# Two AdaLN-like layers, their first three tiles in another order: W0 and x loaded first, the second layer's operands split before the first mixing, late mix blocks copied by ScalarE, no products of ones

## The chip, the cores and the metric

The kernel runs on one core of a Trainium2 chip. The metric is the time on the device of one execution, in microseconds (us). TensorE (PE) multiplies, VectorE (DVE), ScalarE (ACT) and GpSimd (POOL) do the rest, SyncE (SP) issues nearly all DMAs. Every engine works its own list of instructions in order; what they wait for on each other are semaphores written out by hand. All numbers are fp32; where a product needs fp32 accuracy, each operand is split into a high and a low part (type fp32r), and a product is made as hi*hi + hi*lo + lo*hi.

## The reference

Two layers, each adds to x [128, 32, 512] what a feed-forward part makes of a conditioned x:

```
x = x + ffn0(cond0(x))
x = x + ffn1(cond1(x))
cond0: att = softmax(MLP(cond_128));  agg_w[b] = sum_k att[b,k] weight[k]  (32x32 per batch row)
       out[b] = agg_w[b] @ x[b] + (att @ bias_k)[b]
ffn0:  x @ W_base.T + b_base + rank-8 terms of 4 active experts, weighted by a softmax of router logits
cond1: grouped convolution over the 512 positions (9 taps, 4 groups) + (cond_128 @ c_weight.T) + bias
ffn1:  x @ base_W.T + rank-8 terms of the best 2 of 28 experts, weighted by a softmax
```

## The kernel before

**Tiles.** 128 batch rows x 32 channels are 32 tiles of 128 rows (4 batch rows each) and 512 columns. Because `cond0` mixes only within a batch row, the kernel multiplies first and mixes later: `u = x @ [A0 | W0]` per tile (`u_half`, line 1018; half "a" has 292 columns: 36 of the router and rank-8 weights `a0` and 256 of W0, half "b" the other 256), then `mixing` (line 1096) multiplies u by `mix`, a 128x128 block-diagonal matrix of the four `agg_w`. A half of u is 12 products: 8 with x's high part (lines 996, 997) and 4 with its low part (line 1002).

**Steps.** `steps` runs a function `step(s)` on each engine for s = 0 to 33. Step s holds the mixing of tile s, u of a tile further on, the convolution of tile s-1 (`conv`), and layer 2 of tile s-2 (`lows_1`, `base_1`) and s-3 (`low_rank_1`). Steps 0, 1 and 2 are written out apart, step 3 and later are one form. In front of step 0 stands a prologue on every engine:

- SP (lines 361 to 394) loads in this order: `pack` (cond_128, the MLP's weights), `active`, `kw`, x of tile 0, the four chunks of W0, `rows_a`, x of tiles 1 and 2, then four register loads each followed by a DMA of B0's rows, `b_base`, and, when W0 is split (`w0_lo_done`), W1 into the same buffer `w_sb`, `a1`, and so on.
- PE (lines 1028 to 1092): 5 products of ones, the MLP of `cond_128` (`u1_mm`, `u2_mm`, `am_mm`) with `keep_busy` between, which is products of ones again, 18 in all; half b of u of tile 0 chunk by chunk (`first_chunk`) as W0's chunks come; attention, `beta0`; the 8 products `p_mix` that make all `agg_w` (line 1077; 16 passes, since fp32 takes two); column sums of W0 (lines 1008, 1009), half a, more sums, half b of tile 1. Half a of tile 1 stands in step 0, behind the first mixing.
- DVE and ACT share the splits: ACT makes the high part (a cast), DVE the low part (a subtraction). Both copy the blocks of `p_mix` into `mix` for tiles 0 to 3 (`mix_copies`, lines 546 and 739).
- The other 28 tiles' blocks: ACT copies `p_mix` whole to `mix_raw` (`raw_copied`, step 0), POOL copies 16 blocks from there (line 496, steps 1 and 2). POOL also makes the constant rows of the second window buffer (line 463), `z_add` of the 28 tiles (lines 474, 478) and the low part of `b1` (line 513).
- The second layer's operands are split late: `a1` and the first half of W1 in step 1, `b1` and the second half of W1's low part in step 2.

**What links a tile to the next layer.** `residual` (line 827, DVE) makes x1 of a tile; SP stores it (line 417), then loads three shifted windows of it into `win` (line 403); `conv` waits for these.

## Time and profile before

| | us |
|---|---|
| median of 3 runs (390.02 to 390.41) | 390.1 |
| the profiled execution | 389.76 |
| its span, first to last instruction | 388.0 |
| PE busy in it | 376.9 (97%) |
| DVE, ACT, POOL busy | 276.4, 121.1, 41.7 |

The profile is of one execution. Each row of the timeline is an instruction, or several alike one behind the other, with its start, its duration, the operation and what it writes and reads; behind it in brackets the idle time in front of it and what ended that. A product's duration includes the time to run through the array, so products overlap: their pitch is read from start to start. Times at POOL are rough. The span leaves out 1.76 us around the program.

### The profile page before, as it was taken

Reading aid. Unit: us, or ns where it says so; the run is one execution under the profiler, and the core shown is the slowest. Engines: PE = TensorE matmul, PEld = TensorE weight load, DVE = VectorE, ACT = ScalarE, POOL = GpSimd, SP = SyncE. Lnnn points to the kernel's source line nnn. Section 1 sums busy time; section 2 is a strip of 40 time slices with the busy share of each in tenths; the row PEclk is TensorE's granted clock in tenths of the full one; section 3 lists DMA queues with packets and bytes.
Section 4 is the critical chain, followed back from the end, with each engine's and each line's share of the span. In section 5 each row is a group of like instructions: output and inputs, shape, how many; then the busy total and the mean of one; then the engine's idle time right before and its main releaser. Section 6 shows DMA issues by size and latency. Waiting matters only on the chain.

```text
span 388.0 us, 9591 instructions
## 1 busy us (share of the span) xinstructions
PE 376.9 (97%) x3183; PEld 331.3 (85%) x3183; DVE 276.4 (71%) x937; ACT 121.1 (31%) x379; POOL 41.7 (11%) x114
## 2 busy tenths in 40 slices
PE   8999899999999999999999999999999999998986
PEld 7999778888898888888988888889888888887674
DVE  6678997666776676667767767677677666776754
ACT  5266432322333223223332232233322322222211
POOL 2636720000000000000000000000000000000000
PEclk9999999999999999999999999999999999999999
DMA  6765647667777656677776656767766566676631
GB/s 216 256 182 122 161 134 194 175 154 183 162 190 182 141 149 168 153 182 162 190 179 139 157 160 155 187 162 190 180 136 160 160 159 155 139 175 156 164 80 54
DMA packets 71018, 63.05 MB, mean 163 GB/s; under 512 B 4030, under 2 KB 53502, under 8 KB 70872
## 3 DMA queue, kind: packets, MB, share of 16 engines
q1 hardware_dynamic: 70998, 62.82, 64.7%
q8 instruction: 10, 0.16, 0.2%
q14 instruction: 8, 0.07, 0.1%
q10 hardware_dynamic: 2, 0.00, 0.0%
HBM read 45.75 MB, written 16.91 MB: 162 GB/s over the span
## 4 chain that ended last, share of the span: by engine, by line
PE 89%; DVE 5%; DMA 3%; issue 1%; ACT 1%; SPq 1%; DVEq 0%; ACTq 0%
PE p_chy L996 14%; PE p_chy L1002 14%; PE p_chy L997 14%; PE p_u L996 9%; PE p_u L997 8%; PE p_u L1002 8%; PE p_chy L1141 8%; PE p_t L1153 3%; PE p_y L996 2%; PE p_y L1002 2%; PE p_y L997 2%; DMA win<-x_scratch 1%; DMA w_sb<-in_w 1%; PE p_y L1125 1%; PE p_chy L1077 1%
## 5 line engine op out<-in xcount | busy, mean ns | idle before, releaser
L996 PE MATMUL p_u<-w_hi,xt_hi 128*128 128x256 f32 (+1 forms) x256 | 70.5, 302 | 0.8 <-DVE w_lo L729 0.5
L997 PE MATMUL p_u<-w_lo,xt_hi 128*128 128x256 f32 (+1 forms) x256 | 68.1, 292 | 0.0
L835 DVE STREAM_TRANSPOSE c<-p_chy 128x512 f32<-128x512 f32 x32 | 22.9, 716 | 54.2 <-PE p_chy L1141 54.2
L544 ACT CAST u_hi<-p_u 128x256 fp32r<-128x256 f32 x64 | 24.9, 389 | 106.0 <-PE p_u L1002 106.0
L996 PEld LDWEIGHTS p_u<-w_hi,xt_hi 128*128 128x128 f32 x256 | 49.3, 192 | 1.5 <-issue 1.5
L593 ACT CAST g1t_hi<-p_t 112x256 fp32r<-112x256 f32 x32 | 11.9, 373 | 120.7 <-PE p_t L1153 120.7
L997 PEld LDWEIGHTS p_u<-w_lo,xt_hi 128*128 128x128 f32 x256 | 49.4, 193 | 0.0
L996 PE MATMUL p_chy<-w_hi,c_hi 128*128 128x512 f32 x124 | 49.3, 397 | 0.0
L997 PE MATMUL p_chy<-w_lo,c_hi 128*128 128x512 f32 x124 | 48.8, 394 | 0.0
L1002 PE MATMUL p_u<-w_hi,xt_lo 128*128 128x256 f32 (+1 forms) x256 | 43.0, 290 | 0.0
L1002 PEld LDWEIGHTS p_u<-w_hi,xt_lo 128*128 128x128 f32 x256 | 36.6, 190 | 0.0
L1141 PEld LDWEIGHTS p_chy<-win,wc_sb 100*32 100x32 f32 x1024 | 26.0, 109 | 12.3 <-issue 10.6
L1141 PE MATMUL p_chy<-win,wc_sb 100*32 100x128 f32 x1024 | 34.6, 276 | 1.2 <-DMA win<-x_scratch 1.1
L1002 PE MATMUL p_chy<-w_hi,c_lo 128*128 128x512 f32 x124 | 34.0, 396 | 0.0
L996 PE MATMUL p_chy<-a_hi,c_hi 128*128 128x252 f32 x128 | 31.4, 279 | 0.0
L997 PE MATMUL p_chy<-a_lo,c_hi 128*128 128x252 f32 x128 | 31.3, 279 | 0.0
L736 DVE TENSOR_TENSOR u_lo<-p_u,u_hi 128x256 fp32r<-128x256 f32 x64 | 25.6, 434 | 4.4 <-ACT u_hi L544 4.4
L1002 PEld LDWEIGHTS p_chy<-w_hi,c_lo 128*128 128x128 f32 x124 | 23.1, 188 | 5.3
L996 PEld LDWEIGHTS p_chy<-w_hi,c_hi 128*128 128x128 f32 x124 | 23.3, 188 | 4.5 <-issue 0.2
L997 PEld LDWEIGHTS p_chy<-w_lo,c_hi 128*128 128x128 f32 x124 | 23.3, 188 | 4.0
L507 POOL COPY wc_sb<-beta_rows 4x128 f32 (+1 forms) x32 | 9.8, 307 | 154.8 <-PE p_chy L1141 154.5
L996 PE MATMUL p_chy<-b_hi,g1t_hi 112*128 112x512 f32 x62 | 24.9, 402 | 1.4 <-ACT g1t_hi L593 1.4
(166 smaller groups left out, 761.9 us busy)
## 6 DMA issues: line engine op xcount, KB each, us to landing
win<-x_scratch SPq DMA_DIRECT2D x96, 256.0 KB, 4.4
x_scratch<-x SPq DMA_DIRECT2D x32, 260.0 KB, 2.1
xt_sb<-in_xt SPq DMA_DIRECT2D x32, 256.0 KB, 5.1
x_sb<-in_x SPq DMA_DIRECT2D x32, 256.0 KB, 5.1
out<-y_sb SPq DMA_DIRECT2D x32, 256.0 KB, 4.3
w_sb<-in_w SPq DMA_DIRECT2D x4, 256.0 KB, 4.9
w_sb<-in_w SPq DMA_DIRECT2D x1, 1024.0 KB, 5.9
a_sb<-in_a SPq DMA_DIRECT2D x1, 504.0 KB, 7.0
```

The costliest lines, as they stand in the source:

```text
L507: pool.tensor_copy(wc_sb[KIM:KC, s.mod(2)].rearrange("b g (r o) -> b g r o", r=NPH), beta1_rows[KIM:KC, s.n(), :].rearrange("b (g o) -> b ...
L544: nc.scalar.copy(u_hi[:, t.mod(4), cols], p_u[:, banks]).then_inc(u_hi_done[half], 1)
L593: nc.scalar.copy(g1t_hi[:], p_g1t).then_inc(g1t_hi_done, 1)
L736: V.tensor_tensor(u_lo[:, t.mod(4), cols], p_u[:, banks], u_hi[:, t.mod(4), cols].bitcast(f32), ALU.subtract).then_inc(u_lo_done[half], 1)
L835: V.transpose(c1[:], p_cv).then_inc(c1_tr, 1)
L996: mm(psum, lhs_hi, rhs_hi, start=start and n == 0, stop=False)
L997: mm(psum, lhs_hi, rhs_lo, start=False, stop=False)
L1002: last = mm(psum, lhs_lo, rhs_hi, start=False, stop=stop and n == len(operands) - 1)
L1077: last = mm(p_mix[:, m * BATCH:(m + 1) * BATCH], kw_sb[:, m * BT * CH:(m + 1) * BT * CH], att_t[:], start=True, stop=True)
L1125: mm(p_y0[:, ZA + Z0N:ZB], g0t[:], b0_stack[:, 0:NY], start=False, stop=True, skip_group_check=True)
L1141: last = mm(p_cv[rows, :].rearrange("p (b g m) -> p b g m", b=BT, g=GROUPS)[:, :, g], wc_sb[:, v.mod(2), g, :], win[:, v.mod(2)].rearrange ...
L1153: last = nc.tensor.transpose(p_g1t[:, a, :], g1[:, a, :], ident[:])
```

## The change

It moves work in the prologue and in steps 0 to 2; the form of step 3 and later stays.

- Loads: x of tile 0 and W0 first on SP's queue, `pack` on ACT's queue ahead of the router's load; `a1` and `b1` early, W1 as soon as W0 is split; B0's rows, x of tile 0 and `beta1_rows` behind it.
- PE: no products of ones; the MLP's products between W0's chunks; half a of tile 0 ahead of the attention; column sums and `p_mix` behind it; both halves of tile 1 ahead of step 0.
- ACT: splits of `a1`, `b1` and half of W1 in the prologue, copies of the 28 tiles' blocks straight from `p_mix` (`mix_late`, 16 copies of 32 x 224 in steps 0, 1 and 2).
- DVE: low parts of `a1` and `b1` in the prologue, both halves of W1's in step 1, the second window buffer's constant rows in step 2, `z_add` of the 28 tiles at the end of step 2.
- POOL: keeps clearing `mix` (now in one go behind `a0` and `vact`), and two small copies per step.
- `lows_1` of tile 0, which overwrites `p_mix`, waits for the late copies; the convolution of tile 1 and not of tile 0 waits for the constant rows.

The diff, cut (8 columns of indentation taken off):

```diff
 
-    sp.dma_start(pack_sb[:], pack).then_inc(ld_pack, 16)
-    sp.dma_start(act_sb[:], active).then_inc(ld_act, 16)
-    sp.dma_start(kw_sb[:], kw).then_inc(ld_kw, 16)
     load_xt(0)
     for c in W0_ORDER:
         load_w0(c)
+    sp.dma_start(act_sb[:], active).then_inc(ld_act, 16)
     sp.dma_start(rows_sb[:], rows_a.rearrange("p (c e n) -> p c e n", c=HC, e=E0)).then_inc(ld_rows_a, 16)
     load_xt(1)
+    sp.dma_start(kw_sb[:], kw).then_inc(ld_kw, 16)
+    sp.dma_start(a1_sb[:], a1.rearrange("p (c n) -> p c n", c=HC)).then_inc(ld_a1, 16)
     load_xt(2)
+    sp.dma_start(b1_sb[:], b1.rearrange("p (a d) -> p a d", a=2)).then_inc(ld_b1, 16)
+    sp.wait_ge(w0_lo_done, HC)
+    sp.dma_start(w_sb[:], w1.rearrange("p (c d) -> p c d", c=HC)).then_inc(ld_w1, 16)
     sp.wait_ge(ld_act, 16)
...
     sp.dma_start(x_sb[:, 0, :], x_v[0]).then_inc(x_loaded[0], 16)
-    sp.wait_ge(w0_lo_done, HC)
-    sp.dma_start(w_sb[:], w1.rearrange("p (c d) -> p c d", c=HC)).then_inc(ld_w1, 16)
-    sp.dma_start(a1_sb[:], a1.rearrange("p (c n) -> p c n", c=HC)).then_inc(ld_a1, 16)
     load_xt(3)
     sp.wait_ge(ld_rows_b, 16 * ACT0)
     for n in range(1, 3):
         sp.dma_start(b0_raw[n * L0N:(n + 1) * L0N], b0_raw[0:L0N]).then_inc(copied_b, 16)
+    sp.dma_start(x_sb[:, 1, :], x_v[1]).then_inc(x_loaded[1], 16)
+    sp.wait_ge(xt_lo_done, 1)
+    load_xt(4)
     sp.wait_ge(beta1_done, 1)
     for b in range(BT):
         sp.dma_start(beta1_rows[KIM + b:KIM + b + 1], beta1[b:BATCH:BT, :]).then_inc(beta1_moved, 16)
-    sp.dma_start(x_sb[:, 1, :], x_v[1]).then_inc(x_loaded[1], 16)
-    sp.wait_ge(xt_lo_done, 1)
-    load_xt(4)
     for n in range(2):
         sp.dma_start(wc_sb[0:KIM, n], wc.rearrange("k (g n) -> k g n", g=GROUPS)).then_inc(ld_wc, 16)
-    b1_v = b1.rearrange("p (a d) -> p a d", a=2)
-    sp.dma_start(b1_sb[:], b1_v).then_inc(ld_b1, 16)
...
-    zero_mix(range(0, 3))
...
-    pool.wait_ge(ident_done, 1)
-    pool.tensor_copy(win[KIM:KC, 1].rearrange("k (b g) q -> k b (g q)", g=GROUPS),
-                     ident[KIM:KC, KIM:KC].unsqueeze(2).to_broadcast([BT, BT, GROUPS * NQ])).then_inc(batch_rows_done, 1)
-    pool.wait_ge(batch_rows_done, 1)
-    zero_mix(range(3, NT // UNROLL))
-
...
+    zero_mix(range(NT // UNROLL))
...
-            if at(s, 1):
-                pool.wait_ge(raw_act_done, 2)
-                pool.wait_ge(mix_zeroed, NT // UNROLL)
-            if at(s, 1) or at(s, 2):
-                pool.wait_ge(g0_beta_done, s.c + 1)
-                for n in range(2 * s.c - 2, 2 * s.c):
-                    for b in range(BT):
-                        pool.tensor_copy(*raw_blocks(n, b)).then_inc(mix_rest_done, 1)
-                        pool.wait_ge(mix_rest_done, n * BT + b + 1)
-        if at(s, 0):
-            z_rows_rest()
...
-        if at(s, 1):
-            pool.wait_ge(b1_hi_done, 1)
-            pool.wait_ge(wc_beta_done, 2)
-            pool.tensor_tensor(b1_lo[:], b1_sb[:], b1_hi[:].bitcast(f32), ALU.subtract).then_inc(b1_lo_done, 1)
...
+    act.dma_start(pack_sb[:], pack).then_inc(ld_pack, 16)
     act.dma_start(rt_sb[:], router.rearrange("p (a e) -> p a e", a=2)).then_inc(ld_rt, 16)
...
+    def mix_late(n):
+
+        for b in range(BT):
+            nc.scalar.copy(*mix_blocks(REST, n, b)).then_inc(mix_rest_done, 1)
...
     nc.scalar.activation(m1[:], p_mlp, ACT.Gelu, bias=pack_sb[:, C_B0:C_B0 + 1]).then_inc(m1_done, 1)
+    first, second, third = (Tile(None, t) for t in range(3))
+    w0_high(1)
     act.wait_ge(u2_mm, 1)
     nc.scalar.activation(m2[:], p_mlp, ACT.Gelu, bias=pack_sb[:, C_B1:C_B1 + 1]).then_inc(m2_done, 1)
-    act.wait_ge(am_max_done, 1)
-    nc.scalar.activation(am_exp[:], am[:], ACT.Exp, bias=am_max[:], accum_out=am_sum[:]).then_inc(am_exp_done, 1)
-    w0_high(1)
     w0_high(3)
-    first, second, third = (Tile(None, t) for t in range(3))
     xt_high(second)
     act.wait_ge(a0_done, ACT0)
     nc.scalar.copy(w0_hi[:, :, 0:Z0N], a0[:]).then_inc(a0_hi_done, 1)
+    act.wait_ge(am_max_done, 1)
+    nc.scalar.activation(am_exp[:], am[:], ACT.Exp, bias=am_max[:], accum_out=am_sum[:]).then_inc(am_exp_done, 1)
     u_high(first, "b")
-    act.wait_ge(mix_zeroed, 1)
+    act.wait_ge(ld_a1, 16)
+    nc.scalar.copy(a1_hi[:], a1_sb[:]).then_inc(a1_hi_done, 1)
+    act.wait_ge(ld_b1, 16)
+    nc.scalar.copy(b1_hi[:], b1_sb[:]).then_inc(b1_hi_done, 1)
+    u_high(first, "a")
+    xt_high(third)
+    w1_high(0)
+    act.wait_ge(mix_zeroed, NT // UNROLL)
     act.wait_ge(mix_mm, 1)
     mix_copies(FIRST, range(BT // 2))
-    u_high(first, "a")
     mix_high(first)
-    act.wait_ge(rsw0_mm, 1)
-    nc.scalar.copy(b0_raw[3 * L0N:3 * L0N + 3, NY:D], p_rsw0["b"][3 * L0N:3 * L0N + 3]).then_inc(rsw0b_done, 1)
-    xt_high(third)
     u_high(second, "b")
     act.wait_ge(rs0_done, 1)
     nc.scalar.copy(b0_raw[3 * L0N:3 * L0N + 3, 0:NY], p_rsw0["a"][3 * L0N:3 * L0N + 3]).then_inc(rsw0_done, 1)
+    act.wait_ge(rsw0_mm, 1)
+    nc.scalar.copy(b0_raw[3 * L0N:3 * L0N + 3, NY:D], p_rsw0["b"][3 * L0N:3 * L0N + 3]).then_inc(rsw0b_done, 1)
     act.wait_ge(rsw0_done, 1)
     act.wait_ge(rsw0b_done, 1)
     act.wait_ge(ld_rows_b, 16 * ACT0)
     act.wait_ge(copied_b, 16 * 4)
     nc.scalar.copy(b0_round[:], b0_raw[:]).then_inc(b0_round_done, 1)
+    u_high(second, "a")
...
         if at(s, 0):
             z0_exponent(s)
-            raw_copied(0)
-            u_high(s + 1, "a")
+            mix_late(0)
+            u_high(s + 2, "b")
             xt_high(s + 3)
-            u_high(s + 2, "b")
             g0t_copied(s)
-            raw_copied(1)
             u_high(s + 2, "a")
+            mix_late(1)
             xt_high(s + 4)
             mix_high(s + 2)
         elif at(s, 1):
             u_high(s + 2, "b")
             z0_exponent(s)
             u_high(s + 2, "a")
-            act.wait_ge(ld_a1, 16)
-            nc.scalar.copy(a1_hi[:], a1_sb[:]).then_inc(a1_hi_done, 1)
+            w1_high(1)
             xt_high(s + 4)
             u_high(s + 3, "b")
-            w1_high(0)
+            mix_late(2)
             u_high(s + 3, "a")
             g0t_copied(s)
             mix_high(s + 2)
-            w1_high(1)
         elif at(s, 2):
             u_high(s + 3, "b")
-            act.wait_ge(ld_b1, 16)
-            nc.scalar.copy(b1_hi[:], b1_sb[:]).then_inc(b1_hi_done, 1)
+            mix_late(3)
             c1_high(s + -LAG)
             u_high(s + 3, "a")
             z0_exponent(s)
             xt_high(s + 4)
+            mix_high(s + 2)
             t_exponent(s + -LAG)
             g0t_copied(s)
-            act.wait_ge(mix_zeroed, NT // UNROLL)
-            mix_high(s + 2)
...
-    dve.wait_ge(ld_pack, 16)
     w0_high(0, 1)
     w0_low(0)
+    w0_high(2, 2)
+    w0_low(2)
+    xt_low(first)
+    dve.wait_ge(w0_hi_act, 1)
+    w0_low(1)
+    dve.wait_ge(w0_hi_act, 2)
+    w0_low(3)
+    dve.wait_ge(ld_pack, 16)
+    dve.wait_ge(beta1_mm, 1)
+    V.tensor_tensor(beta1[:], p_beta1, pack_sb[:, C_FS:C_FS + CH], ALU.add).then_inc(beta1_done, 1)
     dve.wait_ge(am_mm, 1)
     V.tensor_tensor(am[:], p_am, pack_sb[:, C_B2:C_B2 + MK], ALU.add).then_inc(am_done, 1)
     dve.wait_ge(am_done, 1)
     V.tensor_reduce(am_max[:], am[:], X, ALU.max, negate=True).then_inc(am_max_done, 1)
-    w0_high(2, 2)
-    w0_low(2)
-    xt_low(first)
-    dve.wait_ge(beta1_mm, 1)
-    V.tensor_tensor(beta1[:], p_beta1, pack_sb[:, C_FS:C_FS + CH], ALU.add).then_inc(beta1_done, 1)
+    xt_low(second)
+    dve.wait_ge(a0_hi_done, 1)
+    V.tensor_tensor(w0_lo[:, :, 0:Z0N], a0[:], w0_hi[:, :, 0:Z0N].bitcast(f32), ALU.subtract).then_inc(a0_lo_done, 1)
     dve.wait_ge(am_exp_done, 1)
     V.reciprocal(am_rec[:], am_sum[:]).then_inc(am_rec_done, 1)
     dve.wait_ge(am_rec_done, 1)
     V.tensor_scalar(att[:], am_exp[:], am_rec[:], None, ALU.mult).then_inc(att_done, 1)
-    dve.wait_ge(w0_hi_act, 1)
-    w0_low(1)
+    u_low(first, "b")
     dve.wait_ge(att_t_mm, 1)
     V.tensor_copy(att_t[:], p_att).then_inc(att_t_done, 1)
-    dve.wait_ge(w0_hi_act, 2)
-    w0_low(3)
+    dve.wait_ge(a1_hi_done, 1)
+    V.tensor_tensor(a1_lo[:], a1_sb[:], a1_hi[:].bitcast(f32), ALU.subtract).then_inc(a1_lo_done, 1)
     dve.wait_ge(beta0_mm, 1)
     V.tensor_copy(beta0[:], p_beta0).then_inc(beta0_done, 1)
+    dve.wait_ge(b1_hi_done, 1)
+    V.tensor_tensor(b1_lo[:], b1_sb[:], b1_hi[:].bitcast(f32), ALU.subtract).then_inc(b1_lo_done, 1)
+    u_low(first, "a")
     dve.wait_ge(beta0_done, 1)
...
-    xt_low(second)
-    dve.wait_ge(a0_hi_done, 1)
-    V.tensor_tensor(w0_lo[:, :, 0:Z0N], a0[:], w0_hi[:, :, 0:Z0N].bitcast(f32), ALU.subtract).then_inc(a0_lo_done, 1)
-    u_low(first, "b")
-    dve.wait_ge(mix_zeroed, 1)
-    dve.wait_ge(mix_mm, 1)
-    mix_copies(FIRST, range(BT // 2, BT))
-    u_low(first, "a")
-    mix_low(first)
     dve.wait_ge(vrow_mm, 1)
     V.tensor_copy(vrow[:], p_vrow).then_inc(vrow_done, 1)
     dve.wait_ge(zrow_mm, 1)
     V.tensor_copy(rs0[:], p_rs0).then_inc(rs0_done, 1)
+    dve.wait_ge(mix_zeroed, NT // UNROLL)
+    dve.wait_ge(mix_mm, 1)
+    mix_copies(FIRST, range(BT // 2, BT))
+    mix_low(first)
+    u_low(second, "b")
     dve.wait_ge(rs0_done, 1)
     dve.wait_ge(vrow_done, 1)
     z_rows(FIRST, 1)
-    u_low(second, "b")
...
-            dve.wait_ge(a1_hi_done, 1)
-            V.tensor_tensor(a1_lo[:], a1_sb[:], a1_hi[:].bitcast(f32), ALU.subtract).then_inc(a1_lo_done, 1)
+            w1_low(0)
             u_low(s + 3, "a")
-            w1_low(0)
+            w1_low(1)
         elif at(s, 2):
             u_low(s + 3, "b")
             residual(s + -1)
             c1_transposed(s + -LAG)
-            w1_low(1)
+            V.tensor_copy(win[KIM:KC, 1].rearrange("k (b g) q -> k b (g q)", g=GROUPS),
+                          ident[KIM:KC, KIM:KC].unsqueeze(2).to_broadcast([BT, BT, GROUPS * NQ])).then_inc(batch_rows_done, 1)
             c1_low(s + -LAG)
             z0_logits(s)
             u_low(s + 3, "a")
...
+            z_rows(REST, 2)
+            dve.wait_ge(z_add_done, 2)
...
     pe.wait_ge(ones_done, 1)
-    for _ in range(5):
-        mm(p_u[:, 0:P], ones[:], ones[:], start=True, stop=True)
-
-    pe.wait_ge(ones_r_done, 1)
-
-    def keep_busy(n):
-
-        for _ in range(n):
-            mm(p_u[:, 0:P], ones_r[:], ones_r[:], start=True, stop=True)
-
-    pe.wait_ge(ld_pack, 16)
...
     after(pe, xt_hi_done, first)
     first_chunk(0)
-    keep_busy(6)
+    pe.wait_ge(ld_pack, 16)
+    mm(p_mlp, pack_sb[:, C_W0:C_W0 + P], cond, start=True, stop=True).then_inc(u1_mm, 1)
+    mm(p_beta1, cond, pack_sb[:, C_CW:C_CW + CH], start=True, stop=True).then_inc(beta1_mm, 1)
     first_chunk(1)
-    keep_busy(4)
+    pe.wait_ge(m1_done, 1)
+    mm(p_mlp, pack_sb[:, C_W1:C_W1 + P], m1[:], start=True, stop=True).then_inc(u2_mm, 1)
+    first_chunk(2)
+    first_chunk(3)
+    pe.wait_ge(m2_done, 1)
+    mm(p_am, m2[:], pack_sb[:, C_W2:C_W2 + MK], start=True, stop=True).then_inc(am_mm, 1)
+    after(pe, xt_lo_done, first)
+    lo_passes(p_u[:, banks], u_operands(first, cols), True).then_inc(u_mm["b"], 1)
+    pe.wait_ge(a0_lo_done, 1)
+    u_half(first, "a")
     pe.wait_ge(ident_done, 1)
     pe.wait_ge(att_done, 1)
     nc.tensor.transpose(p_att, att[:], ident[:]).then_inc(att_t_mm, 1)
-    first_chunk(2)
+    pe.wait_ge(vact_done, ACT0)
+    mm(p_vrow, ones[0:1, :], vact[:], start=True, stop=True).then_inc(vrow_mm, 1)
     pe.wait_ge(ld_kw, 16)
     pe.wait_ge(att_t_done, 1)
     for b in range(BT):
         last = mm(p_beta0[by_batch[b]], kw_sb[:, CH * CH:CH * CH + CH],
                   att_t[:].rearrange("k (t b) -> k b t", b=BT)[:, b, :], start=True, stop=True)
     last.then_inc(beta0_mm, 1)
+    pe.wait_ge(ones_r_done, 1)
+    pe.wait_ge(beta1_done, 1)
+    _, cols = HALVES["a"]
+    column_sums(p_cv[:, 0:Z0N + NY], P, w0_hi[:, :, cols], w0_lo[:, :, cols]).then_inc(zrow_mm, 1)
     for m in range(CH // BT):
         last = mm(p_mix[:, m * BATCH:(m + 1) * BATCH], kw_sb[:, m * BT * CH:(m + 1) * BT * CH], att_t[:],
                   start=True, stop=True)
     last.then_inc(mix_mm, 1)
-    first_chunk(3)
-    after(pe, xt_lo_done, first)
-    lo_passes(p_u[:, banks], u_operands(first, cols), True).then_inc(u_mm["b"], 1)
+    u_half(Tile(None, 1), "b")
     pe.wait_ge(beta0_done, 1)
+    _, cols = HALVES["b"]
     column_sums(p_rsw0["b"], P, w0_hi[:, :, cols], w0_lo[:, :, cols]).then_inc(rsw0_mm, 1)
-    pe.wait_ge(a0_lo_done, 1)
-    u_half(first, "a")
-    pe.wait_ge(vact_done, ACT0)
-    mm(p_vrow, ones[0:1, :], vact[:], start=True, stop=True).then_inc(vrow_mm, 1)
-    pe.wait_ge(beta1_done, 1)
-    _, cols = HALVES["a"]
-    column_sums(p_cv[:, 0:Z0N + NY], P, w0_hi[:, :, cols], w0_lo[:, :, cols]).then_inc(zrow_mm, 1)
-    u_half(Tile(None, 1), "b")
+    u_half(Tile(None, 1), "a")
...
-                pe.wait_ge(batch_rows_done, 1)
                 pe.wait_ge(batch_rows_0, 1)
                 pe.wait_ge(rsw0_done, 1)
+            if at(v, 1):
+                pe.wait_ge(batch_rows_done, 1)
...
-                pe.wait_ge(raw_act_done, 2)
+                pe.wait_ge(mix_rest_done, MIX_REST)
...
             mixing(s)
-            u_half(s + 1, "a")
             u_half(s + 2, "b")
```

## Rows read from the trace of the kernel before

**Rows 1.** The page, part 1: busy time, share of the span and instructions of each engine.
```profile
PE 376.9 (97%) x3183; PEld 331.3 (85%) x3183; DVE 276.4 (71%) x937; ACT 121.1 (31%) x379; POOL 41.7 (11%) x114
```

**Rows 2.** Stretches: bounds, length; busy (instructions) of PE, PEld, DVE, ACT, POOL; clock; DMA.
```profile
24.60:52.00 27.40, 25.25 (x227) 22.59 (x226) 25.43 (x61) 15.04 (x39) 17.84 (x26) 1.00 0.53 130
52.00:340.00 288.00, 287.91 (x2512) 254.72 (x2516) 204.84 (x730) 86.00 (x285) 12.23 (x51) 1.00 0.67 165
```

**Rows 3.** Timeline of PE, 24 to 53 us: start, duration, line, names, shapes, count.
```profile
24.67 0.30 PE L996 MATMUL p_y<-u_hi,mix_hi 128*128 128x292 f32 x1
...
25.43 0.30 PE L996 MATMUL p_u<-w_hi,xt_hi 128*128 128x292 f32 x1
...
39.81 1.08 PE L1141 MATMUL p_chy<-win,wc_sb 100*32 100x128 f32 x32
...
52.09 0.40 PE L996 MATMUL p_y<-u_hi,mix_hi 128*128 128x292 f32 x1 [0.16 <-DVE x L827]
```

**Rows 4.** Timeline of PE, 0 to 24.6 us.
```profile
1.07 2.50 PE L1030 MATMUL p_u<-ones 128*128 128x128 f32 x10 [1.07 <-DVE ones L692]
...
12.44 3.78 PE L1077 MATMUL p_chy<-att_t,kw_sb 8*128 8x128 f32 x16
...
16.74 1.05 PE L1002 MATMUL p_u<-w_hi,xt_lo 128*128 128x256 f32 x4
17.59 0.41 PE L1008 MATMUL p_t<-w_hi,ones_r 128*128 128x256 f32 x1
...
19.30 0.45 PE L996 MATMUL p_u<-w_hi,xt_hi 128*128 128x292 f32 x1
...
21.00 0.30 PE L997 MATMUL p_u<-w_lo,xt_hi 128*128 128x292 f32 x1
...
24.20 0.64 PE L1002 MATMUL p_u<-w_hi,xt_lo 128*128 128x256 f32 x4
```

**Rows 5.** Timeline of DVE, 3 to 21 us.
```profile
3.89 1.22 DVE L702 COPY win<-ident 4x2048 f32<-4x2048 f32 x1
...
6.98 0.43 DVE L724 CAST w_hi<-w_sb 128x512 fp32r<-128x512 f32 x1 [1.30 <-DMA w_sb<-in_w]
7.44 0.69 DVE L729 TENSOR_TENSOR w_lo<-w_sb,w_hi 128x512 fp32r<-128x512 f32 x1
...
18.69 1.95 DVE L743 COPY mix<-p_chy 32x32 f32<-32x32 f32 x8
```

**Rows 6.** Timeline of ACT, 18 to 20 us.
```profile
18.10 1.82 ACT L550 COPY mix<-p_chy 32x32 f32<-32x32 f32 x8
```

**Rows 7.** Timeline of DVE, 39 to 45 us.
```profile
39.04 1.22 DVE L749 TENSOR_TENSOR w_lo<-w_sb,w_hi 128x1024 fp32r<-128x1024 f32 x1
...
40.51 0.68 DVE L827 TENSOR_TENSOR x<-p_y,x_sb 128x512 f32<-128x512 f32 x1
...
41.74 2.75 DVE L749 TENSOR_TENSOR w_lo<-w_sb,w_hi 128x1024 fp32r<-128x1024 f32 x1
```

**Rows 8.** Waits, 0 to 60 us: engine, line, releaser; total us, times, longest.
```profile
PE p_chy L1002 <- DVE c_lo L840: 0.8, 1, 0.8
...
PE p_t L1153 <- DVE g L965: 0.5, 1, 0.5
...
PE p_t L1118 <- DVE g0s L871: 0.4, 1, 0.4
...
PEld p_chy L1141 <- DMA win<-x_scratch: 0.3, 1, 0.3
```

**Rows 9.** Timeline of POOL, 29 to 44 us.
```profile
29.75 5.79 POOL L496 COPY mix<-mix_raw 32x224 f32<-32x224 f32 x8 [0.45 <-ACT mix_raw L626]
...
41.00 2.40 POOL L513 TENSOR_TENSOR b_lo<-b_sb,b_hi 112x1024 fp32r<-112x1024 f32 x1 [5.05 <-ACT b_hi L655]
```

**Rows 10.** Timeline of SP, 6 to 32 us: DMA issues and register loads.
```profile
6.86 4.26 SPq L373 DMA_DIRECT2D b_raw<-in_rows_b  x4
...
31.37 0.35 SPq L417 DMA_DIRECT2D x_scratch<-x  x1
```

48 lines of the change are left out of this document (6 added, 42 removed).

## The prediction

> **What bounds the kernel now.** I read the page first, then the stretches, then the products in order of time up to 60 us, then DVE, ACT, POOL and the DMA queue over the same time. The page says that PE is busy 97% of the span [rows 1]. The stretches say where the other 3% are: from 52 to 340 us PE works 287.91 of 288.00 us, between 24.6 and 52 us only 25.25 of 27.40 [rows 2]. The diff leaves the loop's steps 3 and later untouched, and they are a line of products with nothing between them. So the change is worth what it does to one number, the moment at which the mixing of tile 3 starts: 52.09 us [rows 3]. A microsecond gained there is a microsecond gained at the end.
>
> Up to that moment there are two stretches. I call T0 the start of the mixing of tile 0 (24.67 us), and the way from T0 to the mixing of tile 3 the climb: 52.09 - 24.67 = 27.42 us [rows 3].
>
> In the stretch up to T0, PE looks busy, but at which speed? The products tell it. Four of 256 columns start at 16.74 us and the next product at 17.59, so the pitch is 0.85/4 = 0.213 us: 256 columns at 1.2 GHz. Four at 24.20 us are followed at 24.67 [rows 3], 0.118 us each: the 2.4 GHz level. The step lies at 21.00 us, where one of 292 columns takes 0.30 us and not 0.45 [rows 4]. Before it, PE had run products of 256 and 292 columns one behind the other since the mixing passes' end at 12.44 + 3.78 = 16.2 us; these are 16 passes with only 8 rows, and before them it ran mainly products of ones, the first at 1.07 us [rows 4].
>
> **Part 1: the products of ones go.** They lie in time in which PE would wait for W0, and 15 us of them brought no higher clock before 16 us [rows 4]. I take 0 for them. The Trainium skill (TensorE: Matmul & The Clock Gate, Part 1) holds that the array starts throttled and that activity releases it, which speaks against taking them out; the rows disagree, since activity of this kind released nothing. By the page the higher level would come later without them, as in the first of the rivals below.
>
> **Part 2: W0 and x first.** DVE waited until 6.98 us for the first chunk of W0, and its split ended at 7.44 + 0.69 = 8.13 us [rows 5]. Ahead of that chunk stood pack, kw and x, by their shapes in the code 233 + 33 + 256 KB; now x and, on ACT's queue, pack, 256 + 233 KB: nearly the same bytes, so I take 0.1 us. The Trainium skill (DMA: Bandwidth & Descriptors, Issuing engines are not separate DMA queues) says that queues of several engines share the same DMA engines, so that a second queue saves issue time alone; by it this edit gains nothing by the queue. The router's load now stands behind pack on ACT's queue, and DVE waits for it first, with the copy into win (1.22 us, [rows 5]) and the split of x behind; up to 1.3 us of that is covered by the wait that DVE has there today [rows 5]. The chunks 1 and 3 are split by ACT behind the two Gelu steps, whose products now follow the first chunks; with two products and two splits for each I work out the last split at 11.9 us.
>
> **Part 3: the order of PE up to T0.** The first half of u (12 products) starts now at 19.30 us [rows 4]. In front of it stood the 16 mixing passes, 3.78 us, and 8 column sums of 0.213, 1.70 us; both move behind it, so it starts at about 14.1 (19.30 - 5.48 = 13.8, and 0.3 for the attention's steps on DVE, which now stand ahead of the split of a0 that this half waits for). From there PE does, in order, each at the lower or the higher level: the half, 12 products of 292 columns, 2.92 us; attention to beta0, small transposes and copies, some 0.95; 8 column sums, 1.95 or 1.07; mixing passes, 3.78 or about 1.9 (half, an estimate); the next tile's half b, 12 x 0.213 = 2.56 or 1.43; column sums, 1.70 or 0.96; its half a, which before stood behind T0 at 25.43 [rows 3], 2.92 or 12 x 0.134 = 1.60. All low this is 16.8 us, all high behind the first half 10.8.
>
> Everything hangs on when the clock steps up, and the trace of before can't show it. Bounds: if the dense stretch from about 12.8 to 17.1 us is enough, T0 = 14.1 + 10.8 = 24.9; if it comes during the column sums, at 20, they are 0.9 dearer: 25.8. If the step comes as long behind the last mixing pass as in before, 16.2 to 21.0, 4.8 us, the passes end at 14.1 + 2.92 + 0.95 + 1.95 + 3.78 = 23.7 and it comes at 28.5: half b and the sums run low (until 27.95), half a begins low, T0 = 29.8. I take 25.4, the middle of the first two: what PE did before the step of before, products of full width one behind the other, it does here from about 12.8 us on, with breaks of 0.5 and 1 us.
>
> What must be hidden for that: the mix copies that T0 needs (8 on ACT in 1.82 us, 8 on DVE in 1.95, [rows 5, 6]) follow the mixing passes, that end near 21.5; with mix_high and mix_low T0 could be 24.0, so PE has 1 us or more to give. Queued in front of those copies are, on ACT, the splits of a1, b1 and half of w1. The half of w1 waits for 1 MB that is issued once the last split of W0 is done; if it lands later than 20 us, the copies and T0 move with it. A third wait is new in its place: SP's four register loads with their DMAs (4.26 us, [rows 10]), the rows of B0, their copies, x of tile 0 and 1 and beta1 now stand behind w1, and ACT's b0_round waits for the copies with half a of tile 1 queued behind it. From w1's issue at 12 us that is 16.6 for the last load, and by two landings of some 3 us, 23 for the copies; ACT comes there near 25. On DVE stand a1_lo and b1_lo, 1.2 us each by the like split of W1 [rows 7], while PE does its column sums.
>
> **Part 4: the climb.** Removed: half a of tile 1, 1.60 us. Removed with POOL's work: PE waited 0.8 us for c_lo, 0.5 for g and 0.4 for g0s [rows 8]. Why: a split of 1024 columns on DVE takes 1.22 us, but 2.75 when POOL's b_lo (2.40 us from 41.00) runs beside it [rows 7, 9]. It ends 1.09 us after POOL's: it waited. The Trainium skill (SBUF - State Buffer, two separate sides) calls the pair of ports an exclusive lock between the two; the rows agree. In its place between transpose and c_lo comes the copy into win, 1.22 us as in [rows 5]. At the end of step 2, z_rows for 28 tiles comes to DVE, about 1.4 us by [rows 7]; PE covers it as long as it is itself late for the reason that follows.
>
> Added: a new wait. Convolution 0 starts when win has landed: the residual's store is issued at 31.37 and the convolution came at 39.81 after a wait of 0.3 [rows 3, 8, 10], so 8.4 us from store to products. Without half a PE comes 1.6 us earlier, win does not. The residual of tile 0 is done near T0 + 5.65 (its store is now issued at T0 + 6.7; PE's 1.6 us less, but DVE's chain to g0s is 0.5 us longer than what PE does meanwhile) and convolution 0 starts at T0 + 14.1. The residual of tile 1, now started at 40.51 = T0 + 15.84 [rows 7], ended at T0 + 16.5; DVE's work up to it stays (the second split of W1 comes in place of a1's), less 1 us of waits on POOL, so it ends near T0 + 15.5. By the same 8.4 us convolution 1 starts at T0 + 24.0 though PE is ready at T0 + 22.1; then transposes, and the mixing of tile 3 at T0 + 25.4. So the climb shrinks by 2.0 us, not by the 3.3 that the removed work and waits add up to. Bounds: 1.6 (only half a goes) to 3.3 (win lands in time).
>
> The 16 late copies on ACT (32 x 224): no row shows one. Lower bound 0.23 us, from 1.82/8 at 32 columns [rows 6]; upper 0.72, POOL's 5.79/8 for the same blocks [rows 9]. I take 0.35, nearer to ACT's own row. That is 5.6 us on an engine busy 15.04 of 27.40 us there [rows 2], which at the same time gives up the splits of a1, b1 and half of W1. At 0.72 the copy of g0t in step 0 would come some 0.5 us late.
>
> **Sum.** Mixing of tile 3 at 25.4 + 25.4 = 50.8, against 52.09: 1.3 us. The profiled execution took 389.76 us (span 388.0), so 388.5; the median of the runs, 390.1, is 0.34 above it, so 388.8.
>
> **The rivals.**
> - *The clock stays low through the mixing passes (slower).* T0 = 29.8, and with the same climb of 25.4 the mixing of tile 3 starts at 55.2, 3.1 us later: 393.2. For it: in before the clock was low from the first pass to the last and 4.8 us on [rows 4], and now fewer full products stand ahead of the passes than then stood behind them. Against: then the passes came first, and no row shows what a run of full products does before them. It decides from the point at which the clock is still low when the mixing passes begin and stays so to their end.
> - *The step comes at about 21 us, as now (same).* 5 of the 16 passes low, T0 = 26.4, mixing of tile 3 at 51.8, 0.3 us earlier: 389.8. For it: the gains of order are then eaten by slower products.
> - *The climb has no new wait.* T0 = 24.9, climb 24.1, mixing of tile 3 at 49.0: 387.0. For it: win's landing varies; against: the wait of 0.3 us in [rows 8] shows that there is no slack.
>
> **How the numbers follow.** Forecast 0.42, slower rival 0.36, same 0.14, large gain 0.08. This kernel's runs tell about 0.2% (0.8 us) from no change. The forecast's own range is 387.8 to 389.7 (T0 24.9 to 25.8, climb 24.9 to 25.9), of which 0.36 lies beyond 0.2% and 0.06 within; the same-rival gives 0.10 within and 0.02 to each side; the slow rival 0.35 slower and 0.01 within. Faster 0.36 + 0.08 + 0.02 = 0.46, same 0.17, slower 0.37. The range must reach to the slow rival: 387.2 to 393.4.
>
> **What would show it.** Right: first half of u near 14 us; pitch 0.12 us in the column sums or the mixing passes; T0 near 25; c_lo and g0s no longer named as what PE waits for; win named in front of the convolution of tile 1. Wrong: a pitch of 0.213 us still at 24 us; T0 bounded by mix copies or by the load of w1; DVE's first work held up by the router's load behind pack.

## The result: 1.6% slower, and where it went

The changed kernel takes 395.97 us (median of runs from 394.06 to 398.77) where the kernel before, run beside it, takes 390.2: a ratio of 1.016, with an interval from 1.0129 to 1.0191. The forecast was 388.8 us and the range ended at 393.4, so the prediction is wrong in its sign and in its range. The profiled execution took 395.63 us. Its three moments, from [rows 3] and the rows below:

| us | before | after | forecast |
|---|---|---|---|
| T0, mixing of tile 0 | 24.67 | 30.47 | 25.4 |
| mixing of tile 3 (the climb) | 52.09 (27.42) | 56.97 (26.50) | 50.8 (25.4) |
| from there to the last instruction | 335.91 | 336.83 | 335.91 |

Ratios leave out the runs in the chip's slower state (three of e4's ten and two of e7's), while medians and ranges hold all runs.

The page of after, part 1, against [rows 1]: PE works less, POOL much less, and the span is 5.8 us longer.

```profile
span 393.8 us, 9526 instructions
## 1 busy us (share of the span) xinstructions
PE 374.6 (95%) x3155; PEld 328.4 (83%) x3155; DVE 271.5 (69%) x941; ACT 128.7 (33%) x393; POOL 24.3 (6%) x94
```

The timeline of PE in after (start, duration, line, what is written and read, count, in brackets the wait and what ended it), to be read beside [rows 3, 4]: line 1029 is the mixing passes, 952 and 953 the products of u and the mixing.

```profile
14.06 0.61 PE L952 MATMUL p_u<-w_hi,xt_hi 128*128 128x292 f32 x1 [0.22 <-DVE w_lo L733]
...
20.54 3.78 PE L1029 MATMUL p_chy<-att_t,kw_sb 8*128 8x128 f32 x16
...
28.46 0.41 PE L965 MATMUL p_t<-w_lo,ones_r 128*128 128x256 f32 x1
28.68 0.45 PE L952 MATMUL p_u<-w_hi,xt_hi 128*128 128x292 f32 x1
28.92 0.38 PE L953 MATMUL p_u<-w_lo,xt_hi 128*128 128x292 f32 x1
29.13 0.30 PE L952 MATMUL p_u<-w_hi,xt_hi 128*128 128x292 f32 x1
...
30.47 0.30 PE L952 MATMUL p_y<-u_hi,mix_hi 128*128 128x292 f32 x1
...
40.41 0.35 PE L952 MATMUL p_u<-w_hi,xt_hi 128*128 128x256 f32 x1 [0.89 <-DVE u_lo L687]
...
55.77 1.08 PE L1086 MATMUL p_chy<-win,wc_sb 100*32 100x128 f32 x32 [1.45 <-DMA win<-x_scratch]
...
56.97 0.38 PE L952 MATMUL p_y<-u_hi,mix_hi 128*128 128x292 f32 x1
...
59.53 0.73 PE L958 MATMUL p_chy<-b_hi,g1t_lo 112*128 112x512 f32 x2 [0.63 <-DVE g1t_lo L801]
```

The first half of u starts at 14.06 us, as forecast. Then the passes take 3.78 us, the price of before, and the step from 0.45 to 0.30 us, from 1.2 to 2.4 GHz, comes at 29.0 us, 4.7 us behind their end: in before it was 4.8. From 14.06 us to T0 PE waits for no operand, and up to 29.0 it runs at half its clock. The profile's granted clock reads 1.00 over this stretch in both kernels, though the pitch is that of 1.2 GHz; so a level ahead of the first step is read from the pitch, and the granted clock tells later falls. In the climb PE waits for u_lo (0.89 us) and win (1.45), and just behind it for g1t_lo (0.63), where it waited for c_lo, g and g0s [rows 8].

### The profile page after: what moved, and what is told of

Its sections match the earlier page's. It is cut to its first block, busy times and chain, and to the rows that moved or that the text cites. A ratio compares the mean times of both kernels' runs of the same rounds, so it can differ in the third digit from the quotient of the medians.

```text
span 393.8 us, 9526 instructions
## 1 busy us (share of the span) xinstructions
PE 374.6 (95%) x3155; PEld 328.4 (83%) x3155; DVE 271.5 (69%) x941; ACT 128.7 (33%) x393; POOL 24.3 (6%) x94
## 4 chain that ended last, share of the span: by engine, by line
PE 86%; DVE 6%; DMA 3%; ACT 3%; issue 2%; SPq 0%; ACTq 0%; DVEq 0%
PE p_chy L952 14%; PE p_chy L958 14%; PE p_chy L953 14%; PE p_u L952 9%; PE p_u L953 8%; PE p_u L958 8%; PE p_chy L1086 7%; PE p_t L1098 3%; PE p_y L952 2%; PE p_y L958 2%; PE p_y L953 2%; DMA win<-x_scratch 1%; ACT mix L516 1%; PE p_chy L1029 1%; PE p_y L1069 1%
## 5 line engine op out<-in xcount | busy, mean ns | idle before, releaser
L952 PE MATMUL p_u<-w_hi,xt_hi 128*128 128x256 f32 (+1 forms) x256 | 71.9, 307 | 9.8 <-DVE w_lo L680 8.5
L953 PE MATMUL p_u<-w_lo,xt_hi 128*128 128x256 f32 (+1 forms) x256 | 69.0, 295 | 0.0
L952 PEld LDWEIGHTS p_u<-w_hi,xt_hi 128*128 128x128 f32 x256 | 49.9, 195 | 11.5 <-issue 9.4
L494 ACT CAST u_hi<-p_u 128x256 fp32r<-128x256 f32 x64 | 24.9, 388 | 96.5 <-PE p_u L958 96.4
L560 ACT CAST g1t_hi<-p_t 112x256 fp32r<-112x256 f32 x32 | 11.9, 373 | 122.9 <-PE p_t L1098 122.9
L958 PE MATMUL p_u<-w_hi,xt_lo 128*128 128x256 f32 (+1 forms) x256 | 44.2, 296 | 0.0
L958 PEld LDWEIGHTS p_u<-w_hi,xt_lo 128*128 128x128 f32 x256 | 37.5, 195 | 0.0
L952 PE MATMUL p_chy<-b_hi,g1t_hi 112*128 112x512 f32 x62 | 24.9, 402 | 1.4 <-ACT g1t_hi L560 1.4
L953 PEld LDWEIGHTS p_chy<-a_lo,c_hi 128*128 128x128 f32 x128 | 24.2, 189 | 1.3
```

Source lines behind the costliest of these rows:

```text
L494: nc.scalar.copy(u_hi[:, t.mod(4), cols], p_u[:, banks]).then_inc(u_hi_done[half], 1)
L560: nc.scalar.copy(g1t_hi[:], p_g1t).then_inc(g1t_hi_done, 1)
L952: mm(psum, lhs_hi, rhs_hi, start=start and n == 0, stop=False)
L953: mm(psum, lhs_hi, rhs_lo, start=False, stop=False)
L958: last = mm(psum, lhs_lo, rhs_hi, start=False, stop=stop and n == len(operands) - 1)
```

## The experiments

Each was timed beside the kernel before; a time is the median, then the range, then the ratio to before with its interval. A run's own T0 and climb are those of its profile, which is one execution. The diffs are cut, with `...` where lines are left out.

**Products of ones, as they were.** e1 puts them back into after, e2 takes them out of before.

```diff
+            keep_busy(8)
             cond = pack_sb[:, C_COND:C_COND + BATCH]
...
             first_chunk(0)
+            keep_busy(6)
...
             first_chunk(1)
+            keep_busy(4)
```

> The changed kernel with the 5 + 18 products of ones put back (13 ahead of W0's first chunk, 6 behind the first chunk, 4 behind the second). Theory P (the place of the mixing passes keeps the clock low: the step comes some 4.8 us behind the last of them): the clock still steps up near 29 us, the time stays near that of the changed kernel, 395 to 397, 15 or so products of ones more in front cost at most 1 us. Theory O (taking out the products of ones keeps the clock low): the step comes before 24 us and the time falls to 392 or below.

e1: 397.15 us (396.39 to 397.93), 1.0178 (1.0138 to 1.0218), the step at 30.7 us, T0 32.38.

```diff
-            keep_busy(6)
             first_chunk(1)
-            keep_busy(4)
```

> The kernel before without any product of ones. Theory P: no change, 389.8 to 390.6, the clock steps up near 21 us as before, because the mixing passes lie where they lay. Theory O: slower by 2 us or more, with the step later than 24 us.

e2: 390.77 us (389.58 to 393.49), 1.0024 (1.0001 to 1.0047), T0 25.28. What follows: these products, of 128 columns, are worth 0.6 us of T0 in before (one profile each), and in after they only delay. That they are gone is not the loss.

**The order of PE.** e3 moves the passes and the attention in after ahead of half a of tile 0, as in before.

```diff
             last.then_inc(beta0_mm, 1)
+            for m in range(CH // BT):
+                last = mm(p_mix[:, m * BATCH:(m + 1) * BATCH], kw_sb[:, m * BT * CH:(m + 1) * BT * CH], att_t[:],
...
+            pe.wait_ge(a0_lo_done, 1)
+            u_half(first, "a")
```

> The changed kernel with the 16 mixing passes moved ahead of half a of tile 0 (and the attention with them), so that behind them products of full width run unbroken. Theory P: passes end near 19 us, the clock steps up near 24, the mixing of tile 0 starts near 28 and not 30.5, so 2 to 3 us less than the changed kernel: 392.5 to 394. Theory O: the step comes no sooner than 28 us, the time stays within 1 us of the changed kernel.

e3: 396.38 us (395.21 to 396.79), 1.0164 (1.0128 to 1.02). The passes start at 16.60, 4 us earlier, the step comes at 23.8, T0 at 28.67. So the step moves with the passes, though not at a fixed distance: 3.4 us behind their end here, 4.7 in after, about 6 in e2. But most of the 1.8 us was lost again in the climb (27.83): PE waited 1.79 us for win ahead of the convolution of tile 1, and its granted clock was 0.50 from 54.6 to 58.0, behind that wait. Five more profiles show the same dip there (e4, e5, e6, e9 and e14, waits of 1.57 to 1.89 us); those of after, e1, e7 and e8 do not, with 1.45, 1.72, 1.80 and 1.30. What decides it stays open.

**The clock raised early.** e4 puts 16 products of ones of 512 columns ahead of the first chunk in after.

```diff
+            for _ in range(16):
+                mm(p_u[:, 0:D], ones_r[:, 0:P], ones_r[:], start=True, stop=True)
             cond = pack_sb[:, C_COND:C_COND + BATCH]
```

> The changed kernel with 16 products of ones of 512 columns each from 1.4 us on, where PE else waits for W0. Theory W (it is the width: products of 128 columns leave PE's array idle while weights load, those of 512 do not): the clock steps up near 6 us, all products up to 30 us run at the higher level, T0 falls from 30.5 to 22 to 25 us: 387 to 391. If the clock falls back in the breaks between 8 and 14 us, T0 stays near 30 and the time within 1 us of the changed kernel. Theory P says as much as the second of these.

e4: 393.85 us (389.08 to 395.96), 1.0047 (1.0006 to 1.0087). In the profiled execution (395.03 us) the level is high from 8 us, falls at 17.6, comes back at 27.8: T0 28.98. Ahead of the fall PE had waited 1.03 us for att, because of a step of DVE (its timeline):

```profile
13.59 2.34 DVE L738 TENSOR_SCALAR att<-am_exp,am_rec 128x8 f32<-128x8 f32 x1
```

Here it ends as POOL's memsets of mix end (12.12 to 15.90 us). In after they run at the same place (12.06 to 15.86) and it takes 0.35 us. e7 therefore adds to e4 that all memsets come before the first rows.

```diff
+            zero_mix(range(NT // UNROLL))
             pool.wait_ge(ld_act, 16)
...
-            zero_mix(range(NT // UNROLL))
```

> After, with 16 products of ones of 512 columns ahead of the first chunk of W0, and all of POOL's memsets of mix moved to the time before the first rows land, so that PE's break of 1.03 us in front of the attention's transpose (DVE's att took 2.34 us beside the memsets) goes. Theory C (T0 is late because PE runs at 1.2 GHz to 29 us, and the high level, once there, stays as long as PE has no break): the products keep a pitch of 0.12 us through the column sums and the mixing passes, T0 comes at about 25 us (30.47 in after), and the time is about 390.5. Rival (the mixing passes with 8 rows themselves bring the low level): pitch 0.21 us behind the passes, T0 28.5 or later, time 394 or more.

e7: 395.35 us (390.56 to 397.65), 1.0101 (1.0065 to 1.0136), T0 28.00. With the memsets done by 6.25 us, att takes 0.23 us. The clock fell once from 11.8 to 18.7, PE waiting for W0's splits ahead of that. Then the rival held: the passes take 2.31 us, mostly at the high level, and the clock falls again, at 22.1.

**The climb.** e5 moves three steps of DVE in after; e6 moves four late copies of ACT behind what PE needs sooner; e8 is e5, e6 and e7 together.

```diff
                     u_low(s + 2, "a")
+                    z_rows(REST, 2)
                     xt_low(s + 4)
...
+                    residual(s)
                     w1_low(1)
...
-                    residual(s + -1)
```

> After, with three DVE steps moved and nothing else: the copy into win ahead of the mix copies, z_rows of the 28 late tiles into step 0 (where DVE waits 2.11 us for ACT), the residual of tile 1 ahead of the second split of W1. Theory W (in the climb new waits took the place of the removed ones): PE's wait for win ahead of the convolution of tile 1 falls from 1.45 us to about 0.4, that for g1t_lo from 0.63 us to 0, and the time falls by 1.4 to 1.8 us, to about 394.4. Rival (the waits only stand where PE would wait for something else anyway): other waits appear in the same place, the time stays within 0.5 us of after.

e5: 394.59 us (392.87 to 396.81), 1.0094 (1.0067 to 1.0121), T0 30.28. The wait for g1t_lo is gone, that for win is 1.72. The store was issued 1.31 us earlier (47.81 in after), and the windows' loads no more than 0.44 (49.89), as the queue of SP shows: the store took longer to land, and so did the windows. The median came out near the 394.4 us that theory W gave, but its mechanism did not: the profile (396.81 us) has a climb of 27.41, with the dip in it, so the number is no evidence for it.

```profile
46.50 0.34 SPq L406 DMA_DIRECT2D x_scratch<-x  x1
49.45 1.39 SPq L392 DMA_DIRECT2D win<-x_scratch  x3
```

```diff
-                    mix_late(1)
                     xt_high(s + 4)
                     mix_high(s + 2)
+                    mix_late(1)
```

> After, with ACT's second set of four late mix copies (2.30 us) moved behind the split of x and mix_high of step 0. If the copies' size on ACT is what PE waits for at 40.41 us (0.89 us for u_lo, DVE behind ACT's split of x), that wait goes, and if nothing later takes it up the time falls by 0.9 us. Rival: the wait for win ahead of the convolution of tile 1 grows from 1.45 us by what is gained, since its chain hangs on DVE's work and not on PE's: time unchanged. I lean to the rival, with 0.3 us gained.

e6: 396.45 us (392.71 to 398.55), 1.017 (1.0124 to 1.0217). The wait for u_lo halves (0.44), one for g0t of 0.26 is new, that for win is 1.78: the rival's case. Its profile shows more than was asked. Up to T0 its instructions are those of after, and yet (PE's timeline; 964 and 965 are the column sums):

```profile
18.17 0.40 PE L964 MATMUL p_chy<-w_hi,ones_r 128*128 128x292 f32 x1
18.41 0.29 PE L965 MATMUL p_chy<-w_lo,ones_r 128*128 128x292 f32 x1
...
19.44 2.05 PE L1029 MATMUL p_chy<-att_t,kw_sb 8*128 8x128 f32 x16
21.42 0.48 PE L952 MATMUL p_u<-w_hi,xt_hi 128*128 128x256 f32 x1
21.70 0.41 PE L953 MATMUL p_u<-w_lo,xt_hi 128*128 128x256 f32 x1
...
24.69 0.41 PE L965 MATMUL p_t<-w_lo,ones_r 128*128 128x256 f32 x1
24.90 0.32 PE L964 MATMUL p_t<-w_hi,ones_r 128*128 128x256 f32 x1
...
27.02 0.30 PE L952 MATMUL p_y<-u_hi,mix_hi 128*128 128x292 f32 x1
```

In this execution the high level came at 18.2 us, as I had forecast, and the passes took 2.05 us and not 3.78. Then the clock fell, at 21.6, and came back at 25.0. The same instructions thus have a T0 of 30.47 or of 27.02, and the times of after spread over 4.7 us. The profiles of e5 and e14, with the same products up to T0, have the late step (28.7 to 28.8 us) as after has. The Trainium skill (TensorE: Matmul & The Clock Gate, What's actually happening) says that the moment of the step varies between runs of one kernel; these two traces agree, but the page gives ±500 ns for it, and here the steps lie 10.8 us apart.

> The three before together. If C and W both hold, T0 is about 25 us, the mixing of tile 3 starts about 24.8 us behind it at 49.8, against 52.09 in before, and the time is about 388. If the high level is lost at the passes (rival of C): about 392.5. If a break of PE ahead of the convolution of tile 1 brings the low level for some 3 us, 1.5 us more than either.

e8: 392.69 us (389.6 to 394.8), 1.0052 (1.0018 to 1.0086). T0 29.01, climb 25.88: the climb gained 0.6 us on after, the clock fell at 21.0, within the passes, all the same.

**The late mix.** e11 makes this part alone, on before; e14 takes it alone out of after.

```diff
-                    raw_copied(0)
+                    mix_late(0)
...
-                                pool.tensor_copy(*raw_blocks(n, b)).then_inc(mix_rest_done, 1)
```

> Before, with the late mix alone changed: ACT copies the 16 blocks straight out of PSUM and POOL copies none (b_lo and z_rows stay with POOL, the prologue stays). The prediction's prices (0.35 us a copy, waits for g and g0s gone): the climb falls from 27.42 us to about 26.5, time 389.3. With 0.57 us a copy as the profile of after shows, ACT's splits of x and u come later and PE waits some 0.9 us for u_lo in step 0 in place of the waits for g and g0s: climb 27.4, time 390.2.

e11: 395.81 us (395.25 to 396.51), 1.014 (1.0123 to 1.0157), both expectations missed by over 5 us. T0 is 24.54, the climb 32.9, with the clock at 0.5 from 51.2 to 54.6. PE's waits in it, 24 to 60 us (engine, line, releaser; total, times, longest):

```profile
PE p_y L979 <- DVE x L810: 1.7, 1, 1.7
PE p_chy L985 <- DVE c_lo L823: 1.6, 1, 1.6
PE p_y L1108 <- ACT g0t L589: 1.5, 1, 1.5
PE p_u L979 <- ACT xt_hi L506: 1.5, 1, 1.5
```

ACT has the copies beside the splits of a1, b1 and W1 here; in after those of a1, b1 and half of W1 stand ahead of T0. e14:

```diff
-                    mix_late(1)
+                    raw_copied(1)
...
+                                pool.tensor_copy(*raw_blocks(n, b)).then_inc(mix_rest_done, 1)
```

> After, with the late mix as in before (ACT copies PSUM to mix_raw in two pieces of 0.6 us, POOL does the 16 blocks); the rest of after stays. If ACT's copies are what kept the climb at 26.5 us, PE's wait of 0.89 us for u_lo in step 0 goes and the climb falls to about 25.6, less what POOL's copies beside DVE's short steps cost (waits of 0.4 to 0.5 us for g0s and g in before). Rival: the chain to win bounds the climb, 26.5 us whoever copies. The time itself follows T0, which in after lies anywhere from 27 to 30.5 us by the clock.

e14: 392.81 us (391.22 to 395.47), 1.0081 (1.0055 to 1.0108). T0 30.29, climb 26.16, the wait for u_lo 0.36, that for win 1.57. So in after the copies on ACT cost the climb some 0.3 us, win takes up the rest. The time fell by more, but T0's scatter lies in it, so what is owed to the copies stays open.

**The passes woven.** e9 is e7 with two full products behind each two passes; e10 does this in before, whose products of ones it also makes 512 wide (and all of type fp32r); e12 has these wide products alone.

```diff
+                for m in range(CH // BT):
+                    last = mm(p_mix[:, m * BATCH:(m + 1) * BATCH], kw_sb[:, m * BT * CH:(m + 1) * BT * CH], att_t[:],
...
+                    for psum, lhs, rhs, start, stop, done in products[2 * m:2 * m + 2]:
+                        last = mm(psum, lhs, rhs, start=start, stop=stop)
```

> The kernel of e7 (wide products of ones, early memsets) with the 16 mixing passes no longer in one piece: behind each two of them stand two products of 256 columns of the next half b of tile 1 (at the end one half), 12 in all. Theory P (a stretch of 8-row passes alone, 2.0 us at the high level, is what brings the low level back, as at 21.3 us in the profile of e6 and at 22.1 in that of e7): if the high level is there when the weave begins, it stays, the pitch behind it is 0.12 us, and T0 is 25 to 26 us against 28.0 in e7. Rival (the level falls some time after its rise whatever PE does there, or for the narrow products of attention ahead): pitch 0.21 us again within or behind the weave, T0 27.5 or later.

e9: 398.11 us (396.74 to 401.41), 1.0221 (1.0169 to 1.0274), T0 30.88.

> Before, with its 23 products of ones made 512 columns wide (all in fp32r), and the 16 mixing passes woven two by two with the products that follow them there (the last chunk of W0, its four low passes, eight column sums); nothing else. If P holds and the wide products bring the high level ahead of the weave: from 12.6 us passes 2.05, 14 products 1.7, half a 1.6, column sums 1.1, half b 1.4 and 0.2 for vrow, T0 at 21 us against 24.67, and the time 386.5. If the level is low through the weave: T0 at 24.5, time 390.

e10: 392.92 us (391.94 to 394.32), 1.0072 (1.0049 to 1.0095), T0 26.73. In both the clock fell inside the weave (23.7 and 17.2 us). And the weave is dear by itself. Two passes and two products in e10, all at the high level:

```profile
13.60 0.48 PE L1034 MATMUL p_chy<-att_t,kw_sb 8*128 8x128 f32 x2
14.02 0.51 PE L1039 MATMUL p_u<-w_hi,xt_lo 128*128 128x256 f32 x2
14.45 0.48 PE L1034 MATMUL p_chy<-att_t,kw_sb 8*128 8x128 f32 x2
```

0.85 us, where apart they cost 2.05/8 + 2 x 0.12 = 0.50.

```diff
-                    mm(p_u[:, 0:P], ones_r[:], ones_r[:], start=True, stop=True)
+                    mm(p_u[:, 0:D], ones_r[:, 0:P], ones_r[:], start=True, stop=True)
```

> Before, with the wide products of ones alone (no weave), to part the two edits of e10. The level rises early, the passes from 12.4 us run at it in about 2 us in place of 3.78, and then, by P, it falls behind them and comes back some 4 us later, at about 18 us against 21.0: T0 at 22.5 to 23.5 us, time 388.5. Without P the level stays: T0 at 21.5, time 387.

e12: 387.91 us (387.69 to 388.22), 0.993 (0.9914 to 0.9947): faster than both kernels. T0 22.48, climb 27.42 as in before. The passes run high, and behind them the clock falls, from 15.4 to 18.8 us (PE's timeline; 1009 and 1010 are column sums, 997 and 998 half a, and in the last row the mixing):

```profile
12.62 2.05 PE L1077 MATMUL p_chy<-att_t,kw_sb 8*128 8x128 f32 x16
...
15.44 0.42 PE L1009 MATMUL p_t<-w_hi,ones_r 128*128 128x256 f32 x1
15.66 0.41 PE L1010 MATMUL p_t<-w_lo,ones_r 128*128 128x256 f32 x1
...
18.61 0.37 PE L997 MATMUL p_u<-w_hi,xt_hi 128*128 128x292 f32 x1
18.82 0.30 PE L998 MATMUL p_u<-w_lo,xt_hi 128*128 128x292 f32 x1
...
22.48 0.30 PE L997 MATMUL p_y<-u_hi,mix_hi 128*128 128x292 f32 x1
```

**What about the passes brings the low level.** e15 is e12 with ten products of ones in place of the passes (mix then holds constants); e16 keeps the passes and makes their operands 128 rows high, 120 of them zeros.

```diff
-                last = mm(p_mix[:, m * BATCH:(m + 1) * BATCH], kw_sb[:, m * BT * CH:(m + 1) * BT * CH], att_t[:],
+                last = mm(p_mix[:, n % 2 * D:(n % 2 + 1) * D], ones_r[:, 0:P], ones_r[:], start=True, stop=True)
```

> The kernel of e12 without the mixing passes: ten products of ones of 512 columns (2.2 us at the high level) write the same banks instead, so mix holds constants and the output is not the reference's. If the 8-row passes bring the low level back, it does not fall here: pitch 0.12 us from 15 to 22 us, T0 at about 20.9 us against 22.48, time about 386.3. If the level falls there for another reason, T0 stays near 22.5 and the time at 387.9.

e15: 386.27 us (386.16 to 386.68), 0.9923 (0.9897 to 0.9948); no fall, T0 21.21.

```diff
-        kw_sb = sb("kw_sb", [MK, CH * CH + CH])
+        kw_sb = sb("kw_sb", [P, CH * CH + CH])
...
-        att_t = sb("att_t", [MK, BATCH])
+        att_t = sb("att_t", [P, BATCH])
...
+            pool.memset(kw_sb[:], 0.0).then_inc(kw_zeroed, 1)
...
+            V.memset(att_t[:], 0.0).then_inc(att_t_zeroed, 1)
```

> The kernel of e12 with the operands of the mixing passes 128 rows high (120 rows of zeros, written early; the load of kw, 33 KB, moved behind that of the third tile of x). Same columns, same type, same result. If it is the 8 rows that bring the low level back: no fall behind the passes, T0 at 21.2 us as in e15 and 386.3. If it is their type or their 128 columns: low level from 15.3 to 18.6 us as in e12, T0 22.5, 387.9.

e16: 386.00 us (385.67 to 386.51), 0.9914 (0.9889 to 0.9939). PE's timeline:

```profile
12.16 2.05 PE L1082 MATMUL p_chy<-att_t,kw_sb 128*128 128x128 f32 x16
...
14.77 0.28 PE L1014 MATMUL p_t<-w_hi,ones_r 128*128 128x256 f32 x1
14.88 0.28 PE L1015 MATMUL p_t<-w_lo,ones_r 128*128 128x256 f32 x1
...
20.49 0.30 PE L1002 MATMUL p_y<-u_hi,mix_hi 128*128 128x292 f32 x1
```

The same passes, in the same 2.05 us, and the clock stays: T0 is 2.0 us earlier than in e12, of which 0.46 is an earlier start of the passes. In this pair of profiles it is the rows. By the ratios, whose intervals overlap, e16 cannot be told from e12, though its median is the lowest of the study; and of e12's four runs two have a mean granted clock of 0.996, about what 3.4 us at half the clock take off a span of 386, and two 0.999 and 1.000, at times within 0.5 us.

**The second layer's split alone.** e13 is e12 with b1 loaded behind a1 and split ahead of the first mixing (hi on ACT, lo on POOL); e17 loads it ahead of B0's rows; e18 is e17 with the 128 rows.

```diff
             mix_copies(FIRST, range(BT // 2))
+            act.wait_ge(ld_b1, 16)
+            nc.scalar.copy(b1_hi[:], b1_sb[:]).then_inc(b1_hi_done, 1)
             u_high(first, "a")
```

> The kernel of e12 with b1 loaded behind a1 and split ahead of the first mixing (hi on ACT behind its mix copies, lo on POOL ahead of z_rows). PE's wait for c_lo (0.79 us, DVE's split of W1 taking 2.75 us beside POOL's b_lo) goes. If nothing takes its place the climb falls from 27.42 us to 26.6 and the time from 387.9 to 387.1. Rival: the wait for win ahead of the convolution of tile 1 takes it up, since that landed with little to spare; then the time is within 0.3 us of e12.

e13: 391.86 us (389.32 to 392.98), 1.0042 (1.0019 to 1.0065). ACT stood 4.18 us for b1, behind W1 in the queue, with half a's split queued behind it (ACT's timeline), and PE 4.58, behind which its clock was at 0.5 from 24.8 to 31.6 us (T0 27.03):

```profile
23.20 1.04 ACT L574 CAST b_hi<-b_sb 112x1024 fp32r<-112x1024 f32 x1 [4.18 <-DMA b_sb<-in_b]
24.27 0.40 ACT L542 CAST u_hi<-p_u 128x292 fp32r<-128x292 f32 x1
```

This profile also speaks against the 8 rows as the whole cause: the passes have 8 rows, and the level is high ahead of them and stays high behind them, to 24.7 us (PE's timeline; 1007 and 1008 are column sums):

```profile
11.82 0.28 PE L995 MATMUL p_u<-w_hi,xt_hi 128*128 128x256 f32 x1
...
13.95 2.05 PE L1075 MATMUL p_chy<-att_t,kw_sb 8*128 8x128 f32 x16
...
16.74 0.28 PE L1007 MATMUL p_t<-w_hi,ones_r 128*128 128x256 f32 x1
16.86 0.28 PE L1008 MATMUL p_t<-w_lo,ones_r 128*128 128x256 f32 x1
```

```diff
             load_xt(2)
+            sp.dma_start(b1_sb[:], b1.rearrange("p (a d) -> p a d", a=2)).then_inc(ld_b1, 16)
```

> The kernel of e13 with b1 loaded ahead of the rows of B0 and of W1. ACT no longer waits for it, T0 is 22.5 us as in e12. PE's waits for c_lo (0.79), and by POOL's b_lo no longer beside DVE's short steps for g0s (0.45), go in part; the wait for win ahead of the convolution of tile 1 (1.27 us in e13) takes most of it. Mixing of tile 3 at 49.5 to 49.9 us, time 387.5 to 387.9. If win bounds nothing: 48.7 and 386.7.

e17: 386.77 us (386.04 to 387.75), 0.9935 (0.9914 to 0.9956). T0 21.96, climb 26.42. The clock falls behind the passes as in e12, from 15.4 to 18.8. The wait for c_lo fell from 0.79 to 0.19 and those for g and g0s went; that for win is 1.24. In the profile a gain of 1 us in the climb; by the ratios e17 cannot be told from e12.

> Both. If the 8 rows are the cause, T0 at 21.2 us and 385.9 to 386.3; otherwise as e17.

e18: 386.89 us (385.88 to 387.5), 0.993 (0.9907 to 0.9952). No fall, but the load of kw, with that of b1 queued behind it, kept PE waiting 2.22 us (0.23 in e16): T0 22.59.

Taken together: eight profiles reach passes of 8 rows at the high level. Seven lose it in them or behind them (e6 to e10, e12, e17), e13 does not; the three without 8-row passes (e15, e16, e18) keep it. What spared e13 stays open. A rival not tested by itself is the moment of the rise: in e13 the level came between 9.84 and 11.82 us, in e12 and e17 at about 5.2, in e15, e16 and e18 at about 7; e10, with the rise at about 7 and 8 rows, fell all the same, which speaks for the rows. And no run gives after the 128 rows.

## Why the prediction was wrong

The sum erred by 7.1 us on the profiled execution (395.63 against 388.5): T0 5.07, the climb 1.10, the rest behind it 0.92.

**The step that failed is the choice in Part 3**, T0 = 25.4 "the middle of the first two". I weighed when the level rises and took for granted that it then stays. In after it rose only at 29.0, 4.7 us behind the passes. e6 shows the rise where I had put it and the fall behind the passes, so even then T0 is 27.02 and not 24.9 to 25.8. e3 shows that the step moves with the passes; e15 to e18 point to the passes and their rows as what takes the level away, with e13 as an exception whose reason is not shown. The trace of before could have warned: the level came 4.8 us behind the passes there [rows 4], and the rival took this as the rule. Its T0 of 29.8 was the right mechanism. That rival also ended too low, 393.2, since it shared the climb of 25.4: with 0.67 more to T0, 1.10 in the climb and 0.92 behind it, it gives 395.9.

**Part 1**, the ones at 0, held nearly: e2 puts them at 0.6 us of T0, and in e1 they cost 1.9. That PE ran 15 us of them is a misreading: they take 7.0 us, between 1.07 and 11.5. And they were products of 128 columns; in e4 and e12, with products of 512 there, the level was high by 8 us. There the rule of the Trainium skill that I had set aside (TensorE: Matmul & The Clock Gate, Part 1) agrees with the runs: e12 gains 2.2 us of T0 by it.

**Part 2** and the start of **Part 3** held: the last split of W0 ended at 11.71 us, forecast 11.9, and half a started at 14.06, forecast 14.1.

**Part 4, removed**: c_lo, g and g0s at the later step are no longer waited for, and a split of 1024 columns takes 1.22 us where it took 2.75 [rows 7]. **Part 4, win**: the wait came as a mechanism, 1.45 us, but at T0 + 25.3, not T0 + 24.0. The store's way to the convolution took 7.96 us (forecast 8.4); the residual of tile 1 was late, done at T0 + 17.3 and not 15.5 (47.10 + 0.68 in DVE's timeline; the SP line is the store's issue).

```profile
45.63 1.22 DVE L700 TENSOR_TENSOR w_lo<-w_sb,w_hi 128x1024 fp32r<-128x1024 f32 x1
...
47.10 0.68 DVE L782 TENSOR_TENSOR x<-p_y,x_sb 128x512 f32<-128x512 f32 x1
...
47.81 0.34 SPq L406 DMA_DIRECT2D x_scratch<-x  x1
```

Part of its cause is the next term. **Part 4, the late copies**: 0.35 us each was mis-sized. ACT and DVE in after:

```profile
35.97 2.30 ACT L516 COPY mix<-p_chy 32x224 f32<-32x224 f32 x4
38.29 0.62 ACT L476 CAST xt_hi<-xt_sb 128x512 fp32r<-128x512 f32 x1
...
38.95 0.69 DVE L659 TENSOR_TENSOR xt_lo<-xt_sb,xt_hi 128x512 fp32r<-128x512 f32 x1 [2.11 <-ACT xt_hi L476]
```

Four take 2.30 us, 0.57 each: inside my bounds of 0.23 and 0.72, but not the value that I took by the nearest row. DVE stands 2.11 us behind them, and PE 0.89. In e14, with these copies on POOL, the residual is done at T0 + 16.3: they make 1.0 us of its 1.8. The climb gains only 0.3, as the store's way takes 8.54 us there. The other 0.8 us is not traced. **Part 4, z_rows**: "PE covers it as long as it is itself late" failed. Of its two operations the first starts at 56.43 us, and g1t_lo comes only behind them:

```profile
56.43 1.20 DVE L706 TENSOR_TENSOR z_add<-rs,beta 128x1008 f32<-128x1008 f32 x1
57.66 0.38 DVE L710 TENSOR_TENSOR z_add<-z_add,vrow 128x112 f32<-128x112 f32 x1
```

PE waited 0.63 us, which is most of the 0.92; e5 and e8, with them in step 0, have no such wait, and in e8, which has no dip there either, the rest is 335.91 us, as in before.

## What to carry to other kernels

A stretch whose products use few rows of the array can cost twice: in its own time, and in the clock of the full products behind it; where it can't go early, fill its rows with zeros and read in the trace whether the level stays, in more than one profile, since e13 kept it without. A bound on when a clock steps up is no bound until something shows that it stays up. And before work is moved to an engine that the page calls idle, look at what stands behind it there, and price the move by the same shape: 8.8 us of copies on an engine busy 15 of 27 us cost 5 us in one place (e11, a dip of the clock included) and little in another (e14).

## What was not expected of the hardware

- Passes of 8 rows and of 128 rows take the same 2.05 us (e12, e16), and the low level follows the first in e12, for 3.4 us, and not the second; in e13 it does not follow the first either. The Trainium skill (TensorE: Matmul & The Clock Gate, Why this matters for your kernels) says that a product over few rows takes the time of a full one; these runs agree, with 2.05 us for both.
- One program, two clocks: T0 30.47 in after and 27.02 in e6, with the same instructions up to there.
- A change between 8-row fp32 passes and full fp32r products cost 0.17 us each time (0.85 - 0.50 for two, e10).
- DVE's att took 0.23 us where POOL's memsets were over (e7), and beside them 0.35 to 2.34 us (after, e4), in e4 up to their end.
